# Half of the shared expert's first product ahead of the routed experts, and cast matrices written back in two halves, in an eight-core transformer layer

## The reference

```
x = x + attention(layernorm(x))     # 16 heads of 64, causal mask by multiplication, then @ Wr + br
h = layernorm(x)
probs = softmax(h @ router_w + router_b)                  # 8 experts, the best 2 per token are kept
shared = gelu(h @ sw1 + sb1) @ sw2 + sb2                  # 1024 -> 2048 -> 1024
expert_e = gelu(h @ rw1[e] + rb1[e]) @ rw2[e] + rb2[e]    # the same shape, 8 of them
x = x + shared + sum over the chosen experts of probs * expert_e
```

## Time and profile before

| | |
|---|---|
| runs of the kernel before | 1299.67 us median of 3 (1297.54 to 1300.09) |
| the profiled execution | 1299.31 us, of which the span from first to last instruction 1297.7 us, on core 4 |
| spans of the eight cores | 1272.5 to 1297.7 us |
| busy share of the span | PE 88%, ACT 39%, DVE 34%, POOL 17% |
| chain that ended last | PE 69%, DMA 18%, issue 4%, DVE 4% |
| moved by DMA | 235.34 MB, mean 181 GB/s |

### The profile page before, as it was taken

One profiled execution on the slowest core, in us unless ns is written; L12 is line 12 of the kernel. 1 busy time (PEld: TensorE's weight loads), 2 busy tenths in 40 slices (PEclk: granted clock), 3 DMA queues, 4 the chain that ended last, 5 costly groups with the idle time before them and its releaser, 6 DMA issues.

```text
span 1297.7 us, 20995 instructions; the slowest of 8 cores (1272.5 to 1297.7 us)
## 1 busy us (share of the span) xinstructions
PE 1146.6 (88%) x7648; PEld 597.4 (46%) x7648; DVE 447.0 (34%) x617; ACT 503.2 (39%) x669; POOL 224.2 (17%) x389
## 2 busy tenths in 40 slices
PE   5988888678887882199999999999999999999998
PEld 3433332222332341175757575757575744444443
DVE  5457666655665564001010101010101011062346
ACT  5678888677980221131313131313131303312200
POOL 1022320322211005511111111111111102031120
PEclk9999999889998895599999999999999999999999
DMA  7839889888809845599996868585899817072554
GB/s 186 256 130 179 178 200 224 146 200 217 154 2 199 255 163 231 192 192 180 241 232 223 173 214 178 208 175 211 173 192 193 177 57 260 1 259 81 179 171 170
DMA packets 65492, 235.34 MB, mean 181 GB/s; under 512 B 8176, under 2 KB 9072, under 8 KB 64496
## 3 DMA queue, kind: packets, MB, share of 16 engines
q0 software_dynamic: 34592, 123.87, 46.4%
q1 hardware_dynamic: 30800, 110.10, 24.2%
HBM read 235.11 MB, written 76.55 MB: 240 GB/s over the span
## 4 chain that ended last, share of the span: by engine, by line
PE 69%; DMA 18%; issue 4%; DVE 4%; ACT 2%; POOL 2%; another core or an unknown queue 1%; SPq 0%; DVEq 0%; ACTq 0%; POOLq 0%
PE PM L758 20%; PE PM L773 17%; DMA WA<-w2cat 10%; PE PM L711 9%; PE PM L726 9%; DMA wbf<-WA 5%; PE PM L676 3%; PE PM L780 2%; DMA XT<-xtok 2%; POOL WA L454 2%; PE PV L570 1%; PE PV L567 1%; PE TR L737 1%; PE SLOT L611 1%; ACT PT L1134 1%
## 5 line engine op out<-in xcount | busy, mean ns | idle before, releaser
L1134 ACT ACTIVATE PT<-SLOT 128x1024 bf16<-128x1024 f32 (+1 forms) x320 | 262.7, 903 | 62.6 <-PE SLOT L611 61.8
L1059 DVE TENSOR_TENSOR YST<-PM,B2BC 128x512 f32<-128x512 f32 x64 | 44.3, 692 | 475.6 <-PE PM L773 475.6
L1189 ACT ACTIVATE HE_T<-PM,B1ALL 128x576 bf16<-128x576 f32 x128 | 94.9, 741 | 254.1 <-PE PM L758 254.1
L629 PE MATMUL NUM<-PT,VX 128*64 128x512 bf16 (+3 forms) x640 | 117.7, 366 | 34.3 <-POOL PT L472 20.1
L758 PE MATMUL PM<-XET,WA 128*128 128x288 bf16 x1024 | 128.6, 289 | 1.1 <-ACT XET L1174 1.1
L758 PE MATMUL PM<-XET,WB 128*128 128x288 bf16 x1024 | 126.1, 286 | 0.0
L611 PE MATMUL SLOT<-QT,KT 64*128 64x512 bf16 (+3 forms) x640 | 101.9, 360 | 17.4 <-ACT PT L1134 13.7
L636 PE MATMUL DEN<-PT,ONES 128*64 128x512 bf16 (+3 forms) x640 | 112.5, 356 | 4.9 <-DVE DS L873 4.8
L773 PE MATMUL PM<-WA,HE_T 128*128 128x512 bf16 x512 | 114.5, 379 | 0.0
L758 PEld LDWEIGHTS PM<-XET,WA 128*128 128x128 bf16 x1024 | 101.0, 99 | 28.8 <-issue 2.4
L773 PE MATMUL PM<-WB,HE_T 128*128 128x512 bf16 x512 | 113.6, 379 | 0.0
(11 more groups left out here) (116 smaller groups left out, 1014.9 us busy)
## 6 DMA issues: line engine op xcount, KB each, us to landing
WA<-w2cat POOLq DMA_DIRECT2D x56, 512.0 KB, 18.1
wbf<-WA SPq DMA_DIRECT2D x5, 4096.0 KB, 13.6
WA<-w1cat POOLq DMA_DIRECT2D x40, 512.0 KB, 19.8
XT<-xtok SPq DMA_DIRECT2D x32, 512.0 KB, 4.6
WB<-w1cat POOLq DMA_DIRECT2D x32, 512.0 KB, 18.6
yd<-YST SPq DMA_DIRECT2D x32, 512.0 KB, 8.3
WA<-wbf POOLq DMA_DIRECT2D x24, 512.0 KB, 13.7
xe<-ZERO SPq DMA_DIRECT2D x16, 512.0 KB, 6.0
```

Source lines behind the costliest of these rows:

```text
L629: e.matmul(NUM[64 * hh:64 * hh + 64, lo:512], VX[:, kc * D + c * 128 + 64 * hh:kc * D + c * 128 + 64 * hh + 64], pt(n)[:, hh * 512 + lo:(h ...
L1059: e.tensor_add(y[:, h:h + 512], PM2[:, b:b + 512], B2BC[:, h:h + 512]).then_inc(y_ev, 1)
L1134: e.activation(heads(pt(n), lo, 512), heads(slot(r), lo, 512), AF.Exp, scale=0.125).then_inc(expd, 1)
L1189: e.activation(HE_T[:, ht * CAP:(ht + 1) * CAP].rearrange("p (h q) -> p h q", h=2), heads(PM1[:, (n % 2) * 1024:(n % 2 + 1) * 1024], 0, CA ...
```

## The change

- Attention: each early matrix goes through WA1 in two halves with semaphores of their own. SP stores a half when its 4 pieces are in, and POOL reloads a half when its store is done.
- At c = 5 WA1 takes the shared expert's first matrix (w1cat[0]) instead of expert 0's.
- The load of a second matrix at the end of attention is gone. Expert 0's first matrix goes to WB1, issued between the two groups of scatters, its second to WB2, issued behind them. The pairs swap roles for all experts. The number of loads grows by one, as w1cat[0] comes in again for the later half.
- PE does `shared_first(0)` and `shared_first(1)` (256 products) after the logits of the last tile, with `positions(1)` behind the first 40 of them, and ahead of expert 0. Their GELU values go to WA2 and are stored to memory (h1d) in two pieces of 2 MB. The store xsp and its reading back are gone.
- Expert 0's rows are read once all scatters and group 0 are done, the last 64 rows once group 1 is, too.
- At the end the order is first 2, second 0, first 3, second 1, second 2, second 3, with the stored GELU values read back into XLN2T and WA2.

```diff
@@ run_sync
             for k, x in enumerate(EARLY):
-                e.wait_ge(early_in, W_IN * (k + 1))
-                e.dma_start(out=wbf_rows(x, 1), in_=WA1[:]).then_inc(early_out, 16)
+                for h in range(2):
+                    e.wait_ge(early_in[h], W_IN // 2 * (k + 1))
+                    e.dma_start(out=wbf_rows(x, 1)[:, h * 8192:(h + 1) * 8192],
+                                in_=WA1[:, h * 8192:(h + 1) * 8192]).then_inc(early_out[h], 16)
...
-            e.wait_ge(tr_ev, HALF)
-            e.dma_start(out=xsp, in_=XLN2T[:, 0:NCH * 1024]).then_inc(xsp_out, 16)
+            e.wait_ge(s_gelu, 16)
+            spill(e, 0)
...
             e.wait_ge(scat, 16 * 2 * NMT)
-            e.wait_ge(xsp_out, 16)
+            e.wait_ge(s_mm1, 16)
             load_rows(e, 0)
+            e.wait_ge(s_mm1, 32)
+            load_last_rows(e, 0)
+            e.wait_ge(s_gelu, 32)
+            spill(e, 1)
...
+            e.wait_ge(e_mm2, 9 * NE)
             e.wait_ge(y_ev, 9 * NE)
             e.wait_ge(tr_mm, NMT + 5 * NE)
-            e.dma_start(out=XLN2T[:, 0:NCH * 1024], in_=xsp).then_inc(xsp_in, 16)
-
-            e.wait_ge(e_mm2, 9 * NE)
+            e.wait_ge(h1_out, 32)
+            for k in range(AHEAD):
+                e.dma_start(out=hidden(k), in_=h1d[k * 128:(k + 1) * 128, :]).then_inc(h1_in[k], 16)
@@ run_gpsimd
                     if c < len(EARLY):
-                        if c > 0:
-                            e.wait_ge(early_out, 16 * c)
-                        load(WA1, w2cat[EARLY[c] + 1], early_in)
+                        for h in range(2):
+                            if c > 0:
+                                e.wait_ge(early_out[h], 16 * c)
+                            for i in range(PIECES // 2):
+                                piece(WA1, w2cat[EARLY[c] + 1], h * (PIECES // 2) + i, early_in[h])
...
-            e.wait_ge(av_mm, len(SCORES))
-            load(WA2, w2cat[1], w2_in[0])
-
             for g in range(2):
+                if g == 1:
+                    e.wait_ge(op_mm, NMT)
+                    load(WB1, w1cat[1], w1_in[0])
                 e.wait_ge(rt, RT_HALF * g + RT_IDX)
...
-            e.wait_ge(xe_in, 32)
+            e.wait_ge(xn2_done, NMT)
+            for j in range(4):
+                e.wait_ge(x1_out[j], 16 * 4)
+            load(WB2, w2cat[1], w2_in[0])
 
             for x in range(1, NEXP):
                 if x == 1:
-                    e.wait_ge(op_mm, NMT)
+                    e.wait_ge(s_mm1, 32)
                 else:
                     e.wait_ge(e_mm1, 16 * (x - 1))
                 load(w_first(x), w1cat[(x + 1) % NEXP], w1_in[x % 2])
                 if x == 1:
-                    e.wait_ge(xn2_done, NMT)
-                    for j in range(4):
-                        e.wait_ge(x1_out[j], 16 * 4)
+                    e.wait_ge(h1_out, 32)
@@ run_tensor
-            positions(1)
             def shared_first(k):
...
+                    if n == 4:
+                        positions(1)
...
+            shared_first(0)
+            shared_first(1)
             e.wait_ge(rt, RT_END)
             steps = e.value_load(QI[0:1, 0:1])
             for q in range(5):
                 transposes(0, q)
...
             e.wait_ge(w1_in[0], W_IN * 5)
-            shared_first(0)
-            shared_first(1)
+            shared_first(2)
             e.wait_ge(w2_in[0], W_IN * 5)
             shared_second(0)
-            e.wait_ge(xsp_in, 16)
-            shared_first(2)
-            shared_second(1)
             shared_first(3)
-            shared_second(2)
-            shared_second(3)
+            for k in range(1, 4):
+                shared_second(k)
```

More of the change, by code:

```diff
@@ L28 @@
 QS = [128, 128, 128, 128, 64]
-LATE = [2, 3, 0, 1]
-TILES = [4 * tt + i for tt in LATE for i in range(4)]
+AHEAD = 2
 HALF = NMT // 2
@@ L270, in build_program @@
             SB2BC = sb(s, "SB2BC", [128, D], F32)
-        G12, X1D = WB1.ap().bitcast(F32), WB2.ap().bitcast(F32)
+        G12, X1D = WA1.ap().bitcast(F32), WA2.ap().bitcast(F32)
         with ExitStack() as p:
@@ L306, in w_first, with hidden @@
         def w_first(x):
-            return WB1 if x % 2 else WA1
+            return WA1 if x % 2 else WB1
         def w_second(x):
-            return WB2 if x % 2 else WA2
+            return WA2 if x % 2 else WB2
+        def hidden(k):
+            return (XLN2T[:, 0:8192], WA2[:, 8192:16384], H1D[:, 0:8192], H1D[:, 8192:16384])[k]
         def wbf_rows(x, i):
@@ L405, in run_sync @@
                 e.wait_ge(ov_w, 16 * (2 * NE - len(EARLY)))
-                e.dma_start(out=WB1[:], in_=wbf[bass.ds(x * 256, 128), :]).then_inc(ov_in, 16)
-                e.dma_start(out=WB2[:], in_=wbf[bass.ds(x * 256 + 128, 128), :]).then_inc(ov_in, 16)
+                e.dma_start(out=WA1[:], in_=wbf[bass.ds(x * 256, 128), :]).then_inc(ov_in, 16)
+                e.dma_start(out=WA2[:], in_=wbf[bass.ds(x * 256 + 128, 128), :]).then_inc(ov_in, 16)
                 e.dma_start(out=B1X[:], in_=b1cat[bass.ds(x * 128 + 128, 128), :]).then_inc(ov_in, 16)
@@ L698, in run_tensor @@
                     m.then_inc(lg_mm, 1)
-            positions(1)
             def shared_first(k):
+                W = WA1 if k < AHEAD else WB1
                 for ht in range(16):
@@ L705, in shared_first @@
                     if n == 0:
+                        e.wait_ge(x1_done, NMT)
+                        e.wait_ge(s1_in, W_IN)
+                    elif ht == 0 and k == AHEAD:
                         e.wait_ge(e_gelu, 16 * NE)
@@ L724, in shared_second @@
                     for kc in range(16):
-                        at = (k % 2) * 8192 + kc * 512 + (i // 2) * 128
-                        m = e.matmul(psv, H1D[:, at:at + 128], WA2[:, kc * D + (u % 2) * 512:kc * D + (u % 2 + 1) * 512],
+                        at = kc * 512 + (i // 2) * 128
+                        m = e.matmul(psv, hidden(k)[:, at:at + 128],
+                                     WB2[:, kc * D + (u % 2) * 512:kc * D + (u % 2 + 1) * 512],
                                      start=(kc == 0), stop=(kc == 15))
@@ L799, in run_tensor @@
                     for kc in range(NCH):
-                        m = e.matmul(PM1[:, ht * 128:(ht + 1) * 128], WB1[:, kc * DFF + ht * 128:kc * DFF + (ht + 1) * 128],
+                        m = e.matmul(PM1[:, ht * 128:(ht + 1) * 128], WA1[:, kc * DFF + ht * 128:kc * DFF + (ht + 1) * 128],
                                      XET[:, kc * CAP:kc * CAP + 128], start=(kc == 0), stop=(kc == NCH - 1))
@@ L807, in run_tensor @@
                         m = e.matmul(PM2[:, h * 512:(h + 1) * 512], HE_T[:, kc * CAP:kc * CAP + 128],
-                                     WB2[:, kc * D + h * 512:kc * D + (h + 1) * 512], start=(kc == 0), stop=(kc == 15))
+                                     WA2[:, kc * D + h * 512:kc * D + (h + 1) * 512], start=(kc == 0), stop=(kc == 15))
                 m.then_inc(ov_m2, 1)
@@ L1078, in run_vector @@
             e.wait_ge(sb2_in, 16)
-            for i, t in enumerate(TILES):
+            for i in range(NMT):
+                t = i
                 e.wait_ge(d_in[i % 4], 16 * (i // 4 + 1))
@@ L1176, in evacuate_rows @@
                                  AF.Copy).then_inc(tr_ev, 1)
+            e.wait_ge(b1_in, 16)
+            for k in range(AHEAD):
+                shared_gelu(k)
             e.wait_ge(rt, RT_END)
@@ L1208, in run_scalar @@
                 e.reg_add(i, i, 1)
-            for k in range(4):
+            for k in range(AHEAD, 4):
                 shared_gelu(k)
```

69 lines of the change are left out of this document (39 added, 30 removed).

## The result

The changed kernel takes **1287.34 us** (median of 4 runs, 1285.36 to 1289.06) against 1298.61 for the kernel before in the same session: ratio 0.9912, 95% interval 0.9892 to 0.9932. The forecast was 1257. The sign was right, the size a quarter of what was forecast, and the range, 1236 to 1272, ends 15 us ahead of it.

What follows compares the result with a forecast made beforehand. It took casts in attention, output projection stalls and the gap before expert 0 as where time is lost. On core 4, -13.7 - 9.9 + 36.4 - 55.3 = -42.5 gave 1256.8, forecast 1257 us, range 1236 to 1272.

Steps and rivals of the forecast that it cites:

- Bound and places: Time can be had in three places: casts in attention, stalls of the output projection, the gap ahead of expert 0.
- A: Attention: casts in two halves overlap store and load, -13.7 us on core 4, next to nothing on core 0.
- rival 3: Attention gains nothing, loads and stores taking as long beside each other as in turn: 1270 us, chance 0.17.
- B: Output projection: without the load into WA2 beside it, tiles 2 to 6 take 19.8 us instead of 29.7: -9.9 us.
- C: Gap before expert 0: scatters wait behind a matrix, products start 90 us after the last logits: +36.4 us.
- D: End of the kernel: the 256 shared products are gone from it, -55.3 us.
- E: Weights: five matrices queue on POOL, the fifth in before it is needed after two experts, so no stop.
- Rival 1: Gap: scatters aren't held up behind the matrix, products start 67 us after the last logits: 1234 us, chance 0.15.
- Rival 2: Gap: reading the rows shares equally with the cast, 13.5 us instead of 21.2: 1249 us, chance 0.12.
- Rival 5: Experts: the weights' queue becomes the bound at expert 2's first matrix, kernel slower: 1305 us, chance 0.03.
- The signs: Signs of being right: WRF issued near 325 us everywhere, PE idle once about 25 us for XTILE, spans within 12 us.
- The sign for rival 1: In the gap, a PE wait for XTILE under 8 us would show that the scatters weren't held up.

Runs made afterwards that it cites:

- e1: The changed kernel with each early matrix stored whole again instead of in halves: 1281.0 us, ratio 0.9869 to the kernel before.
- e2: The kernel before with only the halves of the early matrices added: 1304.59 us, ratio 1.0062 to the kernel before.
- e11: The kernel before with only the masks changed behind which the casts' loads are issued: 1283.13 us, ratio 0.985.
- e3: The changed kernel with expert 0's first matrix (WB1) loaded behind all 32 scatters instead of between the two groups: 1282.38 us, ratio 0.9881.
- e7: e3 with whole-matrix stores, and SyncE issuing the reads of expert 0's rows ahead of the store of GELU values: 1279.04 and 1274.29 us, two runs.
- e4: e3 with the load into WB1 also waiting until expert 0's first rows are in: 1293.33 us, ratio 0.9972.
- e5: The changed kernel with POOL waiting for both half stores before it issues any load of the next round: 1286.08 us, one run.
- e12: e4 with the second 16 scatters left out, and so the scattering of the last eight tiles' rows: 1287.27 us, one run.

## Why the prediction was wrong

- **Bound and places**: right. All that moved is in attention, the projection, the gap and the end.
- **A (-13.7)**: this is the step that failed. It counted 39 to 40 us a round "if two streams cost no more together than one after the other", and a lag of GpSimd small enough to be free. On core 0 the last three rounds took 42.3, 42.4 and 44.1 us (217.08 to 345.85), the stores there 15.5 to 16.9 us for 2 MB beside a load, and GpSimd stands as long for half a matrix as it had for a whole. Core 4 measured -1.2, and halves by themselves cost 6 to 8 us of the kernel's time (e1, e2). It is rival 3, and a bit worse than its 0: the stated bound "0 if the mixed streams are no faster" left out that they can be slower. The lag was real, and e11 shows what it is worth when it is removed: T of the slowest core falls from 498.9 to 482.9 (another session), 16.0 us, near the 16.7 that A had as its far bound.
- The core by core view misled the sum. Core 4's term was worked out as a gain, core 0's as "next to nothing". It lost 18.7 us and became as slow as core 4.
- **B (-9.9)**: right, 19.75 us against 19.8.
- **C (+36.4)**: mechanism right, mis-sized. On the die without stops products came at T+96.7 instead of T+90: the last scatter was done at T+68.9 on core 0, not T+60 to T+62. The estimate gave the matrix, the first store and the scatters 47 us in turn from T+13; they took 56, with the DMA engines full from T+18 on. The term that was too small is at least in part the store, put at 6.8 us: it costs the scatters 8 to 10 us with no matrix in front (e3 against e7), and on cores 4, 5 and 7, where it is issued only at T+49 to T+59, the rows are asked for at T+54 to T+60. What the matrix took by itself was not separated. Rows (21.69 against 21.2) and transposes (6.2) were right. Core 4 has 4.0 us more, with its stops and the read behind the 2 MB store, 35.36 us, and 5.3 us of stops ahead of T. Nothing in the forecast has them, though the trace of before has such stops on DVE too: the prediction read core 4 alone there and did not compare the dies.
- **D (-55.3)**: -51.7. A pause of 3.09 us ahead of group 2's first product is new (0.40 before); what it is the trace doesn't name.
- **E**: right, PE waited for no weight of experts 0 to 2.
- **Rival 1** (scatters not held): refuted: on core 0 the last scatter, issued at T+36.9, was done at T+68.9. e3's 12 us don't price it, since there the matrix comes later than in rival 1. **Rival 2** (equal shares): twice the time alone would be 13.5 us; measured 21.69. The Trainium skill, DMA: Bandwidth & Descriptors, section Queues, rings and completion order, says that a DMA engine takes turns between queues packet by packet; the trace again disagrees with turns of equal shares. **Rival 3** came true for A, but its 1270 us did not. **Rival 5** did not.
- The signs: WRF near 325 on every core failed at once, PE's wait for XTILE was 32.55 on core 0, not 25, and spans are within 11.4 us as forecast. The sign for rival 1, an XTILE wait under 8 us, would have misled: core 5 has one of 4.14 us, because its PE was late.

The errors on core 4 add up: 12.5 (A), 5.5 (stops in the logits), 10.7 (C), 3.6 (D), 32.3 us in all, which is 1289.06 less 1256.8. A alone would have left the time at 1269, inside the range; the stops, C and D took it out of it.

## What to carry to other kernels

Splitting a transfer to run it beside its neighbour gained nothing here, where the DMA engines' share was 1.00 with the load alone: look at that share first. Where a wait stands in the program order of an engine that others need, move the point of issue instead of the size. Work a slow core's gain out on the fast cores too, since the time is the slowest core's after the change. The indirect writes behind a matrix on the same queue landed late here, and once they were taken out from behind it the matrix itself was the next to wait for.

## What the runs showed that was not expected

- On core 0 of the changed kernel a 2 MB store beside a load took 15.5 to 16.9 us in four rounds of five (8.8 in the first; 6.6 to 18.4 over all cores); a 4 MB store alone took 13.63.
- In every session one die has stops on PE, ACT and DVE between the last logits and expert 0, and the other has next to none (but for one of 7 us on DVE in two cores of e7): cores 4 to 7 for the changed kernel and e1 to e4, cores 0 to 3 for e5 to e12. With the early products there they delay the end of the shared half by 8 to 28 us.
- A reading of 1 MB issued right behind a 2 MB store on the same queue took 35.36 us on core 4 and 29.6 us on core 5 of the changed kernel. It took 21.69 us 37 us behind one (core 0), and 22.6 ahead of one (e7, core 4, where the matrix's load had moved too).
